# Latent attention: plain row maxima from PSUM, the causal mask added by a 128-column TensorE product, long rows joined once per pair

## The reference, cut to what matters

```python
c_kv = x @ Wdkv.T
q = (x @ Wdq.T @ Wuq.T).reshape(B, T, nh, hs).transpose(0, 2, 1, 3)
q_lat = jnp.einsum('bhtd,hdl->bhtl', q, k_eff)
scores = jnp.einsum('bhtl,bsl->bhts', q_lat, c_kv) / jnp.sqrt(jnp.float32(hs))
causal = jnp.tril(jnp.ones((T, T), dtype=bool))
scores = jnp.where(causal[None, None, :, :], scores, jnp.finfo(scores.dtype).min)
attn = jax.nn.softmax(scores, axis=-1)
ctx = jnp.einsum('bhts,bsl->bhtl', attn, c_kv)
y = jnp.einsum('bhtl,hld->bhtd', ctx, v_eff)
```

## Time and profile before

| | |
|---|---|
| median of 3 runs | 920.54 us (917.71 to 920.78) |
| the profiled execution, device time | 920.77 us |
| its span in the trace | 919.0 us |
| granted clock of TensorE, mean over the span | 0.993 of full speed |
| busy: PE, DVE, ACT, POOL | 832.0, 767.2, 606.2, 430.4 us |
| first and last `row_max` operation of VectorE | 667.2 and 824.8 us |

### The profile page before, as it was taken

The page is one execution under the profiler, slowest core; times in us unless marked ns, Lnnn a source line. Parts: engine busy times, 40 slices in busy tenths (PEclk is TensorE's granted clock), DMA queues, the critical chain, the costliest instruction groups (busy, mean ns, idle before and its releaser), DMA issues.

```text
span 919.0 us, 13155 instructions
## 1 busy us (share of the span) xinstructions
PE 832.0 (91%) x4330; PEld 532.6 (58%) x4330; DVE 767.2 (83%) x1597; ACT 606.2 (66%) x1042; POOL 430.4 (47%) x455
## 2 busy tenths in 40 slices
PE   3899999999999999989899999679788999998997
PEld 2555665665665565665466575456655555554686
DVE  3788999889989999999899999676699687876537
ACT  4687767777777676767667777465546767657531
POOL 3134345354446267788668772261323444434301
PEclk9999999999999999999999999899999999999999
DMA  3388859966977767966866677230000000000001
GB/s 123 73 183 159 149 110 189 167 125 135 212 129 151 136 129 139 164 127 138 154 115 115 135 138 152 47 107 1 1 1 1 1 0 2 0 2 1 1 1 46
DMA packets 276867, 86.29 MB, mean 94 GB/s; under 512 B 267584, under 2 KB 272448, under 8 KB 276416
## 3 DMA queue, kind: packets, MB, share of 16 engines
q1 hardware_dynamic: 275520, 80.05, 44.8%
q0 software_dynamic: 992, 5.34, 2.0%
q10 hardware_dynamic: 288, 0.07, 0.1%
HBM read 17.29 MB, written 1.05 MB: 20 GB/s over the span
## 4 chain that ended last, share of the span: by engine, by line
DVE 40%; PE 37%; issue 10%; ACT 8%; DMA 3%; POOL 1%; SPq 0%; POOLq 0%; DVEq 0%; ACTq 0%
DVE EP L1767 9%; DVE nmax L1752 8%; PE ps L1102 6%; PE ps L1104 6%; PE ps L1103 6%; DVE ptm L1866 4%; PE ps L1125 3%; PE ps L1363 3%; DVE ps L1952 3%; PE ps L1349 3%; PE ps L1140 3%; DMA ET<-EP 2%; PE ps L1328 2%; DVE OL L1826 2%; DVE st L1666 2%
## 5 line engine op out<-in xcount | busy, mean ns | idle before, releaser
L1528 ACT ACTIVATE EP<-ps,rinv 128x1024 f16<-128x1024 f32 x128 | 142.3, 1113 | 43.6 <-DVE rinv L1762 41.8
L1767 DVE SCALAR_TENSOR_TENSOR EP<-ps,rinv,EP 128x1024 f16<-128x1024 f32 x128 | 163.3, 1277 | 2.5 <-ACT EP L1528 2.0
L1518 ACT ACTIVATE ps<-ps,nmax 128x1024 f32<-128x1024 f32 x128 | 139.2, 1088 | 35.6 <-DVE nmax L1752 35.1
L1752 DVE TENSOR_REDUCE nmax<-ps 128x1 f32<-128x1024 f32 x128 | 155.0, 1211 | 0.8 <-PE ps L1104 0.8
L1102 PE MATMUL ps<-KH,QH 128*128 128x512 f32 x256 | 115.5, 451 | 7.0 <-DVE KL L1734 4.1
L2111 POOL TENSOR_TENSOR wgu<-wgu,ptm 128x688 f32<-128x688 f32 x60 | 99.7, 1661 | 45.8 <-DVE ptm L1866 43.7
L1102 PE MATMUL ps<-ET,VH 128*128 128x512 f16 x256 | 98.2, 384 | 16.2 <-DMA ET<-EP 12.5
L1104 PE MATMUL ps<-KH,QL 128*128 128x512 f32 x256 | 100.8, 394 | 0.0
L2111 POOL TENSOR_TENSOR wdn<-wdn,ptm 128x512 f32<-128x512 f32 x45 | 57.7, 1281 | 91.9 <-DVE ptm L1866 90.7
L1103 PE MATMUL ps<-KL,QH 128*128 128x512 f32 x256 | 100.5, 392 | 0.0
L1104 PE MATMUL ps<-ET,VL 128*128 128x512 f16 x256 | 98.1, 383 | 0.0
(11 more groups left out here) (250 smaller groups left out, 2125.3 us busy)
## 6 DMA issues: line engine op xcount, KB each, us to landing
wqr<-in_wqk SPq DMA_DIRECT2D x16, 256.0 KB, 3.5
wgu<-in_tern POOLq DMA_DIRECT2D x3, 1024.0 KB, 6.1
wvr<-in_wv SPq DMA_DIRECT2D x8, 256.0 KB, 4.0
wor<-in_wo SPq DMA_DIRECT2D x16, 128.0 KB, 3.2
ET<-EP SPq DMA_TRANSPOSE x128, 4.3
X<-in_x SPq DMA_DIRECT2D x2, 512.0 KB, 6.0
prw<-in_down_idx POOLq DMA_DIRECT2D x2, 256.0 KB, 7.1
tern<-in_l_wuq_rep SPq DMA_DIRECT2D x1, 512.0 KB, 4.3
```

What stands on the lines that cost most here:

```text
L1518: e.activation(bank, bank, ACT.Exp, bias=nmax[:, c:c + 1], scale=1.0, accum_out=rsum[:, c:c + 1]).then_inc(exped.sem, 1)
L1528: e.mul(EP[:, n % NE_RING, 0, :], SB(u, j), rinv[:, c:c + 1]).then_inc(e_hi.sem, 1)
L1752: e.tensor_reduce(nmax[:, c:c + 1], SB(u, j), AX.X, ALU.max, negate=True).then_inc(maxed.sem, 1)
L1767: e.scalar_tensor_tensor(out=EP[:, n % NE_RING, 1, :], in0=SB(u, j), scalar=rinv[:, c:c + 1], in1=EP[:, n % NE_RING, 0, :], op0=ALU.mult, ...
```

## The change

Four things change in latent attention:

1. VectorE's operation of a `row_max` is a plain maximum (`tensor_reduce`) over the part in PSUM. It reads no mask, writes nothing back and has no accumulator to be read out. For i8 below 4 the result goes straight to `NM`, for the others to `M1`, which has a place for each part of two pairs.
2. The mask is added by TensorE: behind the scores of a part that holds the diagonal block, a second product into the same bank, identity (bf16) times mask (bf16), 128 columns wide. There is one for each head and i8, 128 in all. The two bf16 tiles are made once by GpSimd, in a new step `mask_set` in the first feed-forward. The table that is loaded has 128 columns instead of 1024.
3. A new step `join` (p), 8 in all, on VectorE alone: one maximum over the two parts of the 8 long rows of a pair, from `M1` to `NM`. It stands between the two shifts of the pair, with a cost of 0.1.
4. TensorE's transposes of half 1 wait for the `join` instead of for the maxima. The first half is as before.

```diff
     def shifts(p):
-        return [(0.6, ("shift", p, half)) for half in range(2)]
+        return [(0.6, ("shift", p, 0)), (0.1, ("join", p)), (0.6, ("shift", p, 1))]
...
-            M1 = sbuf(ctx, "M1", [P, 32])
+            M1 = sbuf(ctx, "M1", [P, 2, 2, 4, 2])
...
-        mask = tern[:, 0, :].bitcast(F32)
+        mask = tern[:, 0, 0:2 * P].bitcast(F32)
+        maskb, identb = tern[:, 0, 2 * P:3 * P], tern[:, 0, 3 * P:4 * P]
...
-                    e.matmul(ps[:, i, 0:n], QT(p)[:, i8 * P:i8 * P + P], KT[p % 4][:, hh, c:c + n],
-                             start=True, stop=True).then_inc(max_scored.sem, 1)
+                    d = P * i8 - c
+                    mm = e.matmul(ps[:, i, 0:n], QT(p)[:, i8 * P:i8 * P + P], KT[p % 4][:, hh, c:c + n],
+                                  start=True, stop=d >= n)
+                    if d < n:
+                        w.wait_ge(*mask_set["mask"])
+                        w.wait_ge(*mask_set["ident"])
+                        mm = e.matmul(ps[:, i, d:d + P], identb, maskb, start=False, stop=True)
+                    mm.then_inc(max_scored.sem, 1)
                 elif what == "shift":
...
-                    for i8 in range(4 * half, 4 * half + 4):
-                        for hh in range(2):
-                            w.wait_ge(*row_maxed[2 * p + hh, i8, i8 // 4])
+                    if half == 1:
+                        w.wait_ge(*joined[p])
+                    else:
+                        for i8 in range(4):
+                            for hh in range(2):
+                                w.wait_ge(*row_maxed[2 * p + hh, i8, 0])
...
                     w.wait_ge(*max_scored[h, i8, part])
-                    w.wait_ge(*mask_in[0])
+                    if i8 < 4:
+                        w.wait_ge(*zeroed["maxima_zero"])
+                        if p > 1:
+                            w.wait_ge(*m_turned[p - 2, 0])
+                        dst = NM[:, p % 2, i8, 48 + 64 * hh:49 + 64 * hh]
+                    else:
+                        if p > 1:
+                            w.wait_ge(*joined[p - 2])
+                        dst = M1[:, p % 2, hh, i8 - 4, part:part + 1]
+                    e.tensor_reduce(dst, ps[:, BANK[step][0], 0:n], AX.X, ALU.max).then_inc(row_maxed.sem, 1)
+                elif what == "join":
+                    p, = at
                     w.wait_ge(*zeroed["maxima_zero"])
+                    for i8 in range(4, 8):
+                        for hh in range(2):
+                            w.wait_ge(*row_maxed[2 * p + hh, i8, 1])
                     if p > 1:
                         w.wait_ge(*m_turned[p - 2, 1])
-                    if part == 1:
-                        w.wait_ge(*row_maxed[h, i8, 0])
-                    e.tensor_tensor_reduce(src, src, mask[:, m0:m0 + n], 1.0, -3.0e38 if part == 0 else half,
-                                           ALU.add, ALU.max,
-                                           NM[:, p % 2, i8, col:col + 1] if last else half).then_inc(row_maxed.sem, 1)
+                    e.tensor_reduce(NM[:, p % 2, 4:8, 48:113:64].rearrange("p i h -> p h i"), M1[:, p % 2, :, :, :],
+                                    AX.X, ALU.max).then_inc(joined.sem, 1)
...
+                elif what == "mask_set":
+                    w.wait_ge(*mask_in[0])
+                    w.wait_ge(*ident_in[0])
+                    e.tensor_copy(maskb, mask).then_inc(mask_set.sem, 1)
+                    e.tensor_copy(identb, ident[:, :]).then_inc(mask_set.sem, 1)
```

More of the change, by code:

```diff
@@ L258, in order_of_ffn0 @@
     todo += [("norm_in", b1, t) for t in range(4, 8)]
-    todo += [("split_dw",), ("hidden", 5, 0), ("hidden", 6, 0), ("turn_in", b1, 1), ("hidden", 7, 0), ("fold_b",),
+    todo += [("split_dw",), ("mask_set",), ("hidden", 5, 0), ("hidden", 6, 0), ("turn_in", b1, 1), ("hidden", 7, 0), ("fold_b",),
              ("split",), ("down", 0, 0), ("fold_k", 0), ("down", 0, 1), ("fold_k", 1), ("keys_zero", 3), ("fold_v",), ("hidden", 0, 1), ("stats", b2, 0, 0, 4), ("hidden", 1, 1)]
@@ L564, in build @@
             signal(n, "ACT") for n in ("l1_hi", "k_lo_in", "v_set", "weight_exped", "y_copied"))
-        c_split, q_split, k_split_v, row_maxed, q_shifted, y_inv, y_set = (
-            signal(n, "DVE") for n in ("c_split", "q_split", "k_split_v", "row_maxed", "q_shifted", "y_inv", "y_set"))
-        k_split_g, masked = signal("k_split_g", "POOL"), signal("masked", "POOL")
+        c_split, q_split, k_split_v, row_maxed, joined, q_shifted, y_inv, y_set = (
+            signal(n, "DVE") for n in ("c_split", "q_split", "k_split_v", "row_maxed", "joined", "q_shifted", "y_inv",
+                                       "y_set"))
+        k_split_g, masked, mask_set = (signal(n, "POOL") for n in ("k_split_g", "masked", "mask_set"))
         gu_hi, gu_zero_v, gu_lo, dn_hi, dn_lo = (
@@ L869, in build @@
                     dq_lo.mark(m)
+            elif what == "mask_set":
+                mask_set.mark("mask")
+                mask_set.mark("ident")
             elif what in ("values_zero", "maxima_zero"):
@@ L939, in build @@
                 take_ring(step, row_maxed.mark(*at))
+            elif what == "join":
+                joined.mark(*at)
             elif what == "shift":
@@ L1939, in _ @@
                     c, n = cuts(wide)[part]
-                    last = part == len(cuts(wide)) - 1
                     n = min(n, wide - c)
-                    m0, col = 1024 - wide + c, 48 + 64 * hh
-                    src = ps[:, BANK[step][0], 0:n]
-                    half = M1[:, 16 * (p % 2) + 8 * hh + i8:16 * (p % 2) + 8 * hh + i8 + 1]
                     w.wait_ge(*max_scored[h, i8, part])
-                    w.wait_ge(*mask_in[0])
+                    if i8 < 4:
[8 more added lines that the diff above has]
+                    e.tensor_reduce(dst, ps[:, BANK[step][0], 0:n], AX.X, ALU.max).then_inc(row_maxed.sem, 1)
+                elif what == "join":
+                    p, = at
                     w.wait_ge(*zeroed["maxima_zero"])
+                    for i8 in range(4, 8):
+                        for hh in range(2):
+                            w.wait_ge(*row_maxed[2 * p + hh, i8, 1])
                     if p > 1:
                         w.wait_ge(*m_turned[p - 2, 1])
-                    if part == 1:
-                        w.wait_ge(*row_maxed[h, i8, 0])
-                    e.tensor_tensor_reduce(src, src, mask[:, m0:m0 + n], 1.0, -3.0e38 if part == 0 else half,
-                                           ALU.add, ALU.max,
-                                           NM[:, p % 2, i8, col:col + 1] if last else half).then_inc(row_maxed.sem, 1)
+                    e.tensor_reduce(NM[:, p % 2, 4:8, 48:113:64].rearrange("p i h -> p h i"), M1[:, p % 2, :, :, :],
+                                    AX.X, ALU.max).then_inc(joined.sem, 1)
                 elif what == "shift":
@@ L2238, in arrange @@
     r["l1_wot"] = c(rows(wot.reshape(256, 512)))
-    mask = np.zeros((P, 1024), np.float32)
-    mask[:, 896:] = np.where(np.arange(P)[:, None] >= np.arange(P)[None, :], 0.0, NEG)
-    r["mask"] = mask
+    r["mask"] = np.where(np.arange(P)[:, None] >= np.arange(P)[None, :], 0.0, NEG).astype(np.float32)
     pat = np.zeros((P, 16), np.float32)
```

## The result

The changed kernel takes 926.21 us (925.85 to 926.86, 4 runs) against 920.66 us, 5.5 us slower. The ratio is 1.0068 with a 95% interval of 1.0051 to 1.0085; it is an estimate from the single runs and not exactly the quotient of the two medians. Run again beside the last experiments the changed kernel took 930.27 against 920.93 us, 1.0093 (1.0060 to 1.0126). The forecast was 922.5 in a range of 912 to 932.

A forecast was written before the change was run, and what follows sets the result against it. In the latent stretch VectorE and TensorE were taken to set the pace in turns, for 63% and 37% of the maxima. Terms -7.4 + 3.8 + 6.4 - 0.8 = +2.0 us gave 922.5 us, range 912 to 932.

The forecast's parts named there:

- slower: Outcome case for the whole kernel: a time above 925.1 us, given a chance of 0.35.
- The plain maximum: VectorE's 192 row-maximum parts: 0.06 us saved on each, 11.7 us in all, 63% on the path, -7.4 us.
- The mask's products: TensorE's 128 new products: 0.08 us each, 37% of them on the path, +3.8 us.
- The join and the wait for it: Between each pair's shifts: subtraction, join, transposes, subtraction become a chain, eight pairs at 0.8 us, +6.4 us.
- The hand-overs: Between TensorE and VectorE: banks freed 0.15 us earlier, scores handed over later; 8 waits at 0.1 us count, -0.8 us.
- TensorE becomes the bound: Rival: mask products at 0.12 us each, 60% on the path, make TensorE set the pace; +10.4 us, 931 us, chance 0.20.
- VectorE rules: Rival: all 11.7 us of VectorE's saving count and half the joins are covered; -7.6 us, 913 us, chance 0.20.
- No quicker maximum: Rival: on short parts the plain maximum is no quicker than the old operation; +9.4 us, 930 us, chance 0.10.

The follow-up runs named there:

- the join ahead of the shifts: Changed kernel with the join ahead of both shifts of its pair and without the 128 mask products: 918.87 against 919.99 us, ratio 0.9986.
- The last kernel: Kernel before with plain maxima for the 64 parts left of the diagonal, nothing else: 918.40 against 919.99 us, 0.9991; again 918.58 against 920.93, 0.9969.
- the fp32r form: Changed kernel with mask and identity as fp32r tiles instead of bf16: 926.55 against 919.99 us, ratio 1.0074.
- the wait alone: Kernel before plus a 16-element VectorE reduction between each pair's shifts, for which the transposes of half 1 wait: 929.62 against 920.15 us, 1.0089.
- join ahead of both shifts: Changed kernel with the join ahead of both shifts of its pair, mask products kept: 922.52 against 920.15 us, ratio 1.0024.
- reduction, no wait: Kernel before plus the 16-element VectorE reduction between the shifts, transposes waiting for the maxima as before: 921.30 against 920.93 us, 1.0000.

## Why the prediction was right or wrong

The time lies in the range, and on the side to which the forecast leaned, but 4 us from it: +2.0 forecast, +5.5 measured, which passes the border of 925.1 us to "slower", a case that had 0.35. Term by term:

- *The plain maximum, -7.4.* The size of the operation was right: 0.68 us long for 512 columns, where 0.67 was forecast. VectorE's load fell by 8.6 us, of 11.7 forecast. The share of it that counts was wrong. With the join ahead of the shifts it brought 1.3 us by the time and 2.0 by the stretch, about a fifth of VectorE's saving and not 63%; with all of the 2.8 us that TensorE waits there for the join given back it would be 4.8, a share of 56% and still short of 7.4. The last kernel, with plain maxima for 64 parts and no join, shows 1.5 us of stretch for about 3.3 us (64 x 0.05) that VectorE saves, nearly half. So by the stretch the share lies under 63% in each case, between a fifth and somewhat over a half; the times of the last kernel (0.8 and 2.9 us less by the ratio in its two series) are too uncertain to say. The failed step is the one that took the fullest stretches for stretches in which VectorE sets the pace. A stretch that is 91% covered still holds hand-overs, and VectorE's waits for scores rose from 23.2 to 27.2 us when its own step got quicker. The row that said so was there: 23.2 us of waiting for the scores, which I took for the TensorE-paced part alone.
- *The mask's products, +3.8.* Alone +2.6 us by the time and +4.0 by the stretch; right in size, by luck, out of two errors that cancel. Each costs 0.125 us, the upper end of the bounds (0.12) and not 0.08, and a quarter of their time shows in the stretch, not 37%. The estimate of 107 ns that the Trainium skill gave, "TensorE: Matmul & The Clock Gate", section "LDWEIGHTS (loading the stationary operand)", was nearer than 0.08: the fp32r form measures 0.11. Taken out of the changed kernel they gave 1.5 us of stretch back, and put on top of the plain maxima with the join ahead they cost 6.3 (from -2.0 to +4.3). Both differences are bent by the clock, which fell three times in the first without the products, and once, behind pair 0, in the second with them. From pair 2 to 3, 4 to 5 and 6 to 7, where it fell in none of them, they cost 0.7 to 0.9 us each time in every kernel (with the join ahead 0.9, 0.9 and 0.8).
- *The join and the wait for it, +6.4.* The place, the chain and the length were right (0.86 us more for each pair in the changed kernel and 0.94 with the wait alone, against 0.8 and an upper end of 0.95), and that neither engine has anything to put there. Alone it is +8.2 us, and it is the wait and not the join: without the wait the ratio is 1.0000. Missing in the step was that the clock can fall behind such a wait. With the wait alone that cost 3.3 us at four pairs. In the changed kernel it fell once in each profile, for 1.2 us behind pair 0 and 0.3 behind pair 7, and in the fp32r form not at all, so there it is a small part. In the changed kernel moving the join gives 4.1 to 6.4 us back.
- *The hand-overs, -0.8.* Not seen apart from the rest.

By the time the terms add up as far as can be told: alone they are -1.3 + 2.6 + 8.2 = +9.5 us, and measured were 5.5 and 9.3 in two series. By the stretch they come to -2.0 + 4.0 + 10.6 = 12.6 us, against 7.9 and 10.1. Most of that gap is the clock. Without what its falls behind the joins cost it is -2.0 + 4.0 + 7.3 = 9.3 us, against 7.6 and 8.9. The join that is still in the kernel of the first term would lower the sum further; by how much is open.

That the time came out inside the range is in part luck. The gain from the maxima was put some 3 to 6 us too high, the clock was left out, and the slower outcome was covered by the room that the range leaves for the rivals.

The rival "TensorE becomes the bound" was wrong: its price condition came true (over 0.11 us for each product), its path share did not. "VectorE rules" was wrong for the reason of the first term. "No quicker maximum" gave the right gain, nearly nothing, by a wrong reason: the operation is quicker, the kernel hardly. The rule of the Trainium skill, "VectorE: DVE Perf Modes", section "Rules for kernel authors", that tensor_reduce is the slowest operation does not hold against the one replaced here: at 512 columns from PSUM its record is 0.683 us, and that of the old operation 0.723.

## What to carry to other kernels

When a small step is put between two steps of a pipeline over two in-order engines, ask what used to lie beside what: the join cost nothing by its length, and its wait 8 us by making four pieces a chain that had overlapped, while the same join one place earlier leaves the overlap of the subtraction and the transposes and gave back 4 to 6 us. Count a saving on one engine of a coupled pair only as far as an experiment or a chain of waits bears it out; stretches that were covered to 91% passed on about a fifth of it here with a join still in the way, and nearly half without one. And work that an operation does not need (here the mask for parts left of the diagonal) can be left out where it stands, with no new hand-over: that third of the plain maxima, alone, made the kernel before 0.3% faster. And before a difference between two profiles is explained, compare them step by step between instructions that both have: here that told the cost of the wait from the cost of the clock.

## What the runs showed of the hardware

- TensorE's granted clock fell to its lower level, 1.2 GHz, for some 3.5 us at a time in this otherwise full stretch, mostly right behind waits of 1.4 to 2.4 us (pairs 0, 3, 5 and 7 of the kernel with the wait alone, pair 7 of the changed one, pair 0 of the changed one again), but at pair 0 also behind waits of 1.03 us (join ahead of both shifts) and 0.95 us (reduction, no wait), and not behind waits of 2.26 and 2.15 us. A fall cost 0.3 to 1.2 us of time, by the six that two profiles can be laid side by side for. In the two kernels with products that nobody reads in those waits it stayed at 1.00 from 690 to 850 us.
- Two profiles of one kernel agree within 0.1 us over the 124 and the 132 us from pair 1 to pair 7 where the clock does not fall (the version with 64 plain maxima, and the changed kernel).
- A bf16 product of 128 columns with its own weights between fp32 products of 256 columns costs 0.125 us (0.24 to 0.25 from one to the next, less 0.12); in fp32r it costs 0.11 (0.23 less 0.12).
- The record of a plain maximum from PSUM is 0.68, 0.55 and 0.42 us for 512, 384 and 256 columns.
